# An attention and expert kernel on one core: Wk loaded by heads, four PSUM banks for key and value tiles, and the last two head groups run half by half

## What is computed

```python
x = x + tanh(g_xattn) * xattn(layernorm(x), ctx, ctx, pos, mask, Wq, Wk, Wv, Wo)
x = x + tanh(g_ffn) * ffn(layernorm(x), gate_w, gate_b, w1, b1, w2, b2)

# xattn
q, k, v = query @ Wq, key @ Wk, value @ Wv          # by heads
q = q * cos + rotate_half(q) * sin                  # k the same
scores = where(mask == 0, -1e9, q @ k.T / sqrt(D))  # 4 query heads share a key head
return (softmax(scores) @ v) @ Wo

# ffn: 3 experts, top 2, the same two experts for all tokens of a batch
ratio = mean(abs(text rows)) / (mean(abs(vision rows)) + 1e-8)
scores = softmax(concat(h, ratio) @ gate_w + gate_b)
top_val, top_idx = top_k(scores, 2)                 # top_val normalised
act = tanh, gelu, silu of (h @ w1[e] + b1[e]) for e = 0, 1, 2
out = sum over the two slots of top_val * (act[e] @ w2[e] + b2[e]), e = top_idx of token 0
```

## Time and profile before

| | us |
|---|---|
| median of 3 runs | 737.9 |
| lowest and highest of them | 737.53, 738.05 |
| time of the profiled execution | 737.81 |
| its span, first to last instruction | 736.0 |
| PE busy | 704.6 |
| DVE busy | 558.4 |
| POOL busy | 402.6 |
| ACT busy | 357.0 |

### The profile page before, as it was taken

The page is one execution under the profiler, slowest core; times in us unless marked ns, Lnnn a source line. Parts: engine busy times, 40 slices in busy tenths (PEclk is TensorE's granted clock), DMA queues, the critical chain, the costliest instruction groups (busy, mean ns, idle before and its releaser), DMA issues.

```text
span 736.0 us, 11337 instructions
## 1 busy us (share of the span) xinstructions
PE 704.6 (96%) x3478; PEld 587.7 (80%) x3478; DVE 558.4 (76%) x924; ACT 357.0 (49%) x955; POOL 402.6 (55%) x340
## 2 busy tenths in 40 slices
PE   5798899899999999999999999999999879999998
PEld 3686688688888888888888888888888766788886
DVE  4977778778878787878888887878787984378832
ACT  5522452455554545454545545454545574872130
POOL 5653524665766666666657566666666541383020
PEclk9999999999999999999999999999999999999999
DMA  8695465432133131212213112222222310240101
GB/s 285 223 288 204 171 216 185 129 101 64 52 87 87 58 87 57 82 61 72 71 36 109 58 56 86 86 57 87 58 77 67 104 69 29 58 115 14 58 1 58
DMA packets 66111, 71.10 MB, mean 97 GB/s; under 512 B 8592, under 2 KB 42384, under 8 KB 66064
## 3 DMA queue, kind: packets, MB, share of 16 engines
q1 hardware_dynamic: 65680, 69.51, 30.1%
q0 software_dynamic: 384, 1.05, 0.4%
HBM read 51.66 MB, written 18.87 MB: 96 GB/s over the span
## 4 chain that ended last, share of the span: by engine, by line
PE 82%; DVE 6%; issue 5%; ACT 3%; POOL 3%; DMA 1%; SPq 0%; POOLq 0%; ACTq 0%; DVEq 0%
PE q L263 34%; PE y L253 28%; PE o L590 5%; PE s L542 5%; PE pt L464 4%; PE s L544 2%; PE o L253 1%; PE pt L253 1%; ACT prob L840 1%; POOL roped L1033 1%; DVE rot L1141 1%; DVE rot L1142 1%; DVE rot L1140 1%; DMA wraw<-in_L_xattn_Wk 1%; POOL scores L1033 1%
## 5 line engine op out<-in xcount | busy, mean ns | idle before, releaser
L263 PE MATMUL q<-xT_hi,big 128*128 128x512 f32 x704 | 235.9, 400 | 0.4 <-issue 0.4
L253 PE MATMUL y<-big,split 128*128 128x512 f32 (+1 forms) x784 | 193.0, 392 | 2.9 <-DVE split L1113 2.9
L253 PEld LDWEIGHTS y<-big,split 128*128 128x128 f32 x784 | 147.9, 189 | 34.5 <-DVE split L1113 3.9
L263 PEld LDWEIGHTS q<-xT_hi,big 128*128 128x128 f32 x704 | 132.2, 188 | 27.3 <-issue 0.6
L263 PE MATMUL q<-xT_lo,big 128*128 128x512 f32 x352 | 136.9, 389 | 0.0
L1060 POOL TENSOR_TENSOR roped<-rot 128x512 f32<-128x512 f32 x59 | 76.4, 1295 | 104.1 <-DVE rot L1142 104.1
L840 ACT ACTIVATE prob<-scores,nmax 128x128 f32<-128x128 f32 x256 | 99.8, 391 | 22.2 <-DVE nmax L1245 22.2
L828 ACT ACTIVATE big<-roped 128x512 fp32r<-128x512 f32 x64 | 40.5, 633 | 142.3 <-POOL roped L1060 137.6
L1076 POOL TENSOR_TENSOR prob<-prob,prec 128x512 f32<-128x512 f32 x64 | 66.6, 1040 | 50.7 <-DVE prec L1259 50.7
L1064 POOL TENSOR_TENSOR big<-roped,big 128x512 fp32r<-128x512 f32 x64 | 82.8, 1294 | 13.4 <-ACT big L828 13.4
L1052 POOL TENSOR_TENSOR big<-wraw,big 128x512 fp32r<-128x512 f32 x64 | 83.2, 1300 | 1.9 <-ACT big L820 1.9
(11 more groups left out here) (170 smaller groups left out, 1141.9 us busy)
## 6 DMA issues: line engine op xcount, KB each, us to landing
k_scratch<-split SPq DMA_DIRECT2D x16, 512.0 KB, 3.5
v_scratch<-split SPq DMA_DIRECT2D x16, 512.0 KB, 3.6
wraw<-in_L_xattn_Wq SPq DMA_DIRECT2D x32, 256.0 KB
wraw<-in_L_xattn_Wo SPq DMA_DIRECT2D x32, 256.0 KB
kv<-k_scratch SPq DMA_DIRECT2D x64, 128.0 KB, 2.5
kv<-v_scratch SPq DMA_DIRECT2D x64, 128.0 KB, 2.8
wraw<-in_L_ffn_w SPq DMA_DIRECT2D x28, 256.0 KB
rows<-ctx_t SPq DMA_DIRECT2D x8, 256.0 KB
```

Source lines behind the costliest of these rows:

```text
L253: mm = pe.matmul(bank_[:, :], stationary(s, c), moving(m, c), start=(c == 0 and n == 0), stop=(c == EC - 1 and n == 2))
L263: mm = pe.matmul(bank_[:, :].rearrange("p (b t) -> p b t", b=BH), weights[s][:, c, h * P:(h + 1) * P], source[m][:, half * BH:(half + 1) * ...
```

## The change

Six things change together.

1. Wk comes in a layout with one chunk per head (`wk_t`, made on the host as the context is), so a key tile needs one chunk and not four. The order of loads at the start becomes w0, c0 to c3, w1, w2, w3.
2. Keys up to K9 rotate over four banks (q0, q1, pt, o), values up to V9 over four (y0, y1, and the two halves of s). The rope tables are transposed through the halves of s, behind K1 and not behind K0.
3. The first phase has 26 tiles, keys earlier; six value tiles, V10 to V15, follow in units 1 to 6. In unit 6 the first `pt` stands behind the query and the value tile.
4. `LN_AT` and `X_AT` move with the tiles.
5. The last two head groups run half by half: units 48 to 51 are group 6 for batches 0 to 3, 52 to 55 group 7 for the same batches, 56 to 63 the same for batches 4 to 7. The weights come in the order of `TAIL_CHUNKS`.
6. So batches 0 to 3 are finished earlier: their statistics stand in units 60 to 63, their rows in 61 to 64, their transposes in 64 and 65. Four first-layer tiles stand in units 67 to 70, fl4 to fl7 behind the drain with the router behind fl7, token 0 behind fl9.

```diff
-TILE_ORDER = "KKVKVKV" * 4 + "VVVV"
-TILES_A = 28
-VALUES_IN = (1, 2, 3, 4)
+TILE_ORDER = "KKKVKVKV" + "KKVKV" * 3 + "KKV" + "VVVVVV"
+TILES_A = 26
+VALUES_IN = (1, 2, 3, 4, 5, 6)
+KEYS_WIDE = 10
+VALUES_WIDE = 10
-LN_AT = (9, 11, 13, 16)
-X_AT = 20
+LN_AT = (8, 10, 12, 14)
+X_AT = 18
+TAIL = UNITS - 2 * B
+TAIL_CHUNKS = dict(zip(range(TAIL, UNITS), (
+    (68,), (69,), (70, 71), (72,), (73,), (74,), (75,), (76,), (77,), (78,), (79,), (), (80,), (81,), (82,), (83,))))
+H_STAT = {60: 0, 61: 1, 62: 2, 63: 3, 68: 4, 69: 5, 70: 6}
+H_ROW = {61: 0, 62: 1, 63: 2, 64: 3, 69: 4, 70: 5}
+H_TURN = {64: (0, 1), 65: (2, 3), 69: (4,), 70: (5,)}
+H_SPLIT = {65: (0, 1), 66: (2, 3), 70: (4,)}
+H_ABS = {64: (0,), 65: (1, 2), 66: (3,), 70: (4,)}
+FIRST_AT = {67: 0, 68: 1, 69: 2, 70: 3}
...
+        def key_bank(n):
+            return (qbank + [pbank, obank])[n % 4] if n < KEYS_WIDE else qbank[n % 2]
+
+        def value_bank(n):
+            return (ybank + [sbank, tbank])[n % 4] if n < VALUES_WIDE else ybank[n % 2]
...
+        def place(i):
+
+            if i < TAIL:
+                return i // B, i % B
+            t = (i - TAIL) // BH
+            return KVH - 2 + t % 2, t // 2 * BH + i % BH
...
+        def last_unit(hb):
+            return TAIL + BH + hb + (hb >= BH) * BH
...
                 if keys:
-                    if n >= 2:
-                        pe.wait_ge(k_rot, n - 1)
+                    if bank_user(key_bank, n) is not None:
+                        pe.wait_ge(k_rot, bank_user(key_bank, n) + 1)
...
+            first_layer(EC)
             h_transpose(B - 2)
-            first_layer(2)
+            first_layer(EC + 1)
             h_transpose(B - 1)
-            first_layer(3)
+            first_layer(EC + 2)
             gate_products(1)
-            for l in range(EC, NX * EC):
-                first_layer(l)
-                if l == EC:
-                    router()
-                if l == EC + 2:
-                    token0()
+            first_layer(EC + 3)
+            router()
+            first_layer(2 * EC)
+            first_layer(2 * EC + 1)
+            token0()
+            first_layer(2 * EC + 2)
+            first_layer(2 * EC + 3)
```

More of the change, by code:

```diff
@@ L300, in slot_a @@
         def slot_a(m):
-            slots = [k % NST for k in range(4 * B - 1)] + [0]
+            slots = [k % NST for k in range(4 * B - 2)] + [0, 0]
             return slots[m], slots[:m].count(slots[m])
@@ L413, in unit @@
                 i = g * B + b
-                if not drain and past >= EC:
+                if isinstance(g, int) and TAIL <= i < UNITS:
+                    for n in TAIL_CHUNKS[i]:
+                        w_load(n, tail_chunk(n)).then_inc(w_in[n % NW], 16)
+                elif not drain and past >= EC:
                     n = g * W_PER + (W_A + b)
@@ L504, in _ @@
                 ready = None
-                if n == 0:
-                    ready = chunk_ready(first, 0 if keys else None)
-                elif keys and n == HG:
-                    ready = chunk_ready(None, EC)
+                if keys:
+                    pe.wait_ge(w_lo, first + k % HG + 1)
+                    if n in (0, HG):
+                        ready = chunk_ready(None, n // HG * EC)
+                elif n == 0:
+                    ready = chunk_ready(first, None)
                 elif k == 0:
@@ L592, in unit @@
                     mm.then_inc(o_done, 1)
-                if drain and b >= 1:
-                    h_transpose(b - 1)
-                if drain and b == LAG_Y - 2:
-                    first_layer(0)
+                if isinstance(g, int):
+                    for hb in H_TURN.get(i, ()):
+                        h_transpose(hb)
             def h_transpose(hb):
@@ L745, in tile_hi @@
                     act.wait_ge(v_proj, n + 1)
-                    act.activation(split[:, slot, 0, :], ybank[n % 2][:, :], ACT.Copy).then_inc(u_hi, 1)
+                    act.activation(split[:, slot, 0, :], value_bank(n)[:, :], ACT.Copy).then_inc(u_hi, 1)
             def rope_copy(k):
@@ L808, in unit @@
                     act.activation(split[:, 2, 0, :], obank[:, :], ACT.Copy).then_inc(o_hi, 1)
-                if not drain:
+                if isinstance(g, int) and TAIL <= i < UNITS:
+                    for n in TAIL_CHUNKS[i]:
+                        w_tail_hi(n)
+                elif not drain:
                     if b == 0 and past >= B:
@@ L1060, in unit @@
                         pool.tensor_tensor(roped[:, :], rot[:, 0, :], rot[:, 1, :], ALU.add).then_inc(q_roped, 1)
-                        if not drain:
+                        if isinstance(g, int) and TAIL <= i < UNITS:
+                            for n in TAIL_CHUNKS[i]:
+                                w_split_lo(n, *tail_target(n))
+                        elif not drain:
                             weight_lo()
```

259 lines of the change are left out of this document (165 added, 94 removed).

## The result

The changed kernel takes 742.07 us (median of 4, 741.74 to 742.32), the kernel before beside it 737.71 (736.69 to 738.05). The ratio is 1.0067 (95% interval 1.0048 to 1.0086): 4.4 us slower where 3.7 faster was forecast. The profiled execution took 741.91 us.

The account below looks back on a forecast made before the run. PE is busy 704.6 of 736.0 us, so only the two ends matter; a chain DVE, POOL, ACT, DVE bounds the first phase. Start, units 60 to 63 and drain: 737.81 - 3.7 + 0.2 - 0.1 = 734.2; range 729.0 to 737.5.

Parts of the forecast that it names:

- What bounds the kernel: Whole kernel: PE busy 704.6 of 736.0 us, no gap from unit 8 to 64, so only the two ends matter.
- Wk by heads: Start of first phase: first rotation at 20.2 where it was 19.46; no gain, 0.7 lost.
- three keys first: First phase: K4's rotation at 41.8 where it was 43.39, with PE idling some 7.6 us around K4.
- 1.2 GHz: Start of first phase: PE still slow, K0 ending near 11.8 at 0.43 us a matmul, K1 near 16.3.
- half a slow tile: After 3.0 of idleness at the first row transpose: low clock would cost 1.4, half counted, unit 0 at 100.5.
- Contention beside POOL: DVE in the first phase: key and context parts beside POOL's work take 1.7 us each, alone 0.69.
- Entry into the units: Unit 0 to unit 8: 45.5 of work and waits of 1.4 and 0.5, 47.5; start gains 3.7 in all.
- the `o` wait: Unit 6: PE waits 1.4 us for `o`, whose low part needs ACT and DVE right behind the late `pt`.
- The drain: Unit 64 to second layer: waits 12.0 to 13.1 against 13, 95.5 to 96.6 us against 96.18; no gain, 0.1.
- fl11: Behind the drain: PE waits 4.3 us between fl10 and fl11, 3.2 if the small DVE steps run freely.
- rival (b): Behind the drain: picks do not hold fl11 up, 4.3 less, so 730; chance 0.18 together with another rival.
- (d): First phase: PE stays at the low clock round K4, K4 at 46.5, phase 4.7 later than summed: 739.6; chance 0.08.

Follow-up runs that it names:

- chunk_first: The changed kernel with the weight chunks of units 4 to 7 issued by SP one unit earlier: 1.0021 of the kernel before.
- store_ahead: chunk_first with DVE's low part of the last value tile, V15, made ahead of the rotation in unit 7: 0.9994 of the kernel before.
- best_start: The kernel before with the new first phase alone, the steps of chunk_first and store_ahead, and V2 and V3 ahead of K4: 0.9954 of the kernel before.
- old_order: The changed kernel with the old first phase, leaving Wk by heads and the last two groups half by half: 1.0055 of the kernel before.
- tail_fixed: old_order with the order of steps behind the drain of ahead_drain4: 0.9967 of the kernel before.
- drain_order: The changed kernel with, behind the drain, fl9's activation ahead of the first kept tiles and picked tiles ahead of expert chunks: 1.0068 of the kernel before.
- warm_k4: store_ahead with 27 extra matmuls in the three waits for K4's context parts: 0.9984 of the kernel before, 735.70 us.
- ahead_drain4: store_ahead with the third version behind the drain: two picks before kept tiles, a wait narrowed to one low part, an earlier activation: 0.9935, 731.99 us.
- best_b: ahead_drain4 with V2 and V3 ahead of K4, and DVE's low part of a key tile behind the next key's rotation: 0.9935 of the kernel before.
- values_early: The changed kernel with the last six value tiles one unit earlier, in units 0 to 5: 1.0001 of the kernel before, 736.29 us.

## Why the prediction was wrong, step by step

- **What bounds the kernel: right.** Only the two ends matter; 56 units take 421.29 us (153.58 to 574.87), of which 1.7 is the slow stretch in unit 8.
- **Wk by heads and three keys first: right, on the cautious side.** The first rotation came at 18.70 (forecast 20.2), K4's at 40.12 (41.8), unit 0 at 99.55 (100.5). PE was not slow as long as forecast: K0 and K1 were through at 14.4, for 16.3. The table by stretches gives a granted clock of 1.00 from 6.5 to 14 in both kernels, so the "1.2 GHz" of the prediction for K0 is not what its rows show, though the first 15 matmuls took 5.81 us, 0.39 each, and the next 9 took 0.23 each. PE idled at K4, 6.9 us (7.6), at the first row 2.39 (3.0), at K10 0.99 (2.8). Of the 0.7 counted for half a slow tile nothing came.
- **Contention beside POOL: held.** Four parts took 1.75 to 1.78 us between 25.0 and 34.6, as in the earlier trace rows. That is what the rule of the Trainium skill's page "SBUF — State Buffer" ("Who interferes with whom") has for a DVE instruction with two inputs in SBUF beside a GpSimd instruction that reads SBUF; the trace agrees with these four.
- **Entry into the units: wrong, and this gave the sign of the trace.** Forecast 47.5 from unit 0 to unit 8, measured 54.0, and 1.7 more in unit 8. The failed step is the sum for this stage. It had PE's tiles and the two waits that PE's own chain makes (the `o` wait came as said: 1.41). It took for granted that everything else moves with unit 0. SP's queue did not. I had costed six value tiles in the units on PE and DVE, and not the store that each issues, nor what stands behind it on SP. chunk_first and store_ahead show both: 1.0067 to 0.9994. With the two waits gone the start gives what was forecast for it: 3.4 us in best_start (where V2 and V3 are moved too), for 3.7.
- **The drain: the sum right in the trace, the step wrong in the median.** Unit 64 to the second layer took 96.54, forecast 95.5 to 96.6. But the waits sum to 8.0 and not 12 to 13. In the trace of the kernel before they sum to 7.7 and not 13, so its 96.18 us are 88.4 of work with one slow stretch, and not 83: the split was misread there already, and by luck the two errors cancel in the difference. And old_order shows that this part costs 4 us over all executions, where the prediction has "no gain, 0.1". The missing term is what the order of steps behind the drain costs over all executions (6.5 us less without it, by tail_fixed), some of it waits and some low clock: I counted the low clock for the first phase, at half, and not at all for the drain.
- **fl11: the mechanism right, 2.16 for 3.2 to 4.3.** fl6 waited 1.28 for 1.5. The chain from the copy behind token 0 to the end of fl9's activation took 4.8 us (650.33 to 655.17) where 7.2 had been summed. Its small DVE steps took 1.7, for 3.6 before; rival (b) had them at 2 or more. The activation started 1.30 after the table load again (632.03 to 633.33, as in the earlier trace rows). The drain of about 1.38 us that the Trainium skill's page "ScalarE: Activation LUTs" ("What ACT_TABLE_LOAD costs") adds to the load was not seen.
- **The rival that ended slower (d) had the wrong place.** It put the loss at K4; K4 came 1.7 us early. A rival with its price in SP's queue was missing.
- **Rival (b)**, that the picks don't hold fl11 up, would have been worth little anyway: drain_order took that wait away and 3.70 stood at the next tile.

What stays open: warm_k4 and the traces say that waits bring the low clock, but not when. The wait at unit 8 was followed by it in 2 of 6 traces (after 1.61 and 1.77; not after 1.55, 1.57, 1.66 and 1.84). Those two are the only traces with the longer wait at unit 5 (2.21 and 2.11), which the low clock followed as well. And 2.5 of tail_fixed's 6.5 us are not in its trace against old_order's; its mean clock (0.9898 for 0.9867) is 4.6 us less at half speed, worth up to 2.3: most of them, but no trace here shows where.

## What to carry to other kernels

If a stage is made to start earlier, list for each wait at its entry who ends it, and follow that engine's or queue's own list back. A load that is issued in order behind stores moves only as far as those stores do. When one engine goes through a fixed list, removing one wait shows the next: here the third version behind the drain was the first to gain time, so judge such a fix by the sum of waits to the end of the stage. And one trace shows one draw of the clock; the mean granted clock over all executions tells whether a part costs more than its trace says.

## What was not expected of the hardware

- In these traces, the end of the kernel aside, the stretches at the low clock are 3.41, 6.83, 10.24 or, once, in ahead_drain4, 13.65 us long, and a tile that meets one takes 4.21 to 5.25 us (best_b) for 2.72.
- The same kernel spends different times at it: the mean clock of best_start's 8 executions goes from 0.988 to 0.993. values_early takes 734.9 us on average at 0.991 (4 executions) and 737.6 at 0.986 (3), 2.7 us for a difference of 0.005, which is 3.7 us of PE time.
